# Moving copies, loads and late projections between queues and slots in a four-layer sandwich kernel

## The reference, cut to what matters

```
x = x + layernorm(layer(layernorm(x)))
```

```
gate = silu(lin(x, w1q, a1, b1)); up = lin(x, w3q, a3, b3); y = lin(gate * up, w2q, a2, b2)
lin(x, wq, A, B) = x @ tile(wq, (1, 4)).T + 0.5 * x @ A.T @ B.T
```

```
q = x @ Wq; k, v = x @ Wkv; w = softmax(causal(q k^T) / sqrt(32)); y = (w v) @ Wo + bo
```

## Time and profile before

| | |
|---|---|
| Median of three runs (lowest, highest) | 2157.19 us (2152.95, 2161.05) |
| The profiled execution | 2154.8 us, span 2153.0 us |
| TensorE busy, granted clock | 2002.1 us (93%), 0.973 of full |
| VectorE, GpSimd, ScalarE busy | 1423.2 (66%), 1064.7 (49%), 933.4 us (43%) |
| DMA | 292 MB, mean 136 GB/s |

### The profile page before, as it was taken

The page is one execution under the profiler, slowest core; times in us unless marked ns, Lnnn a source line. Parts: engine busy times, 40 slices in busy tenths (PEclk is TensorE's granted clock), DMA queues, the critical chain, the costliest instruction groups (busy, mean ns, idle before and its releaser), DMA issues. The chain is left out here.

```text
span 2153.0 us, 30681 instructions
## 1 busy us (share of the span) xinstructions
PE 2002.1 (93%) x10444; PEld 1451.0 (67%) x10444; DVE 1423.2 (66%) x3201; ACT 933.4 (43%) x1938; POOL 1064.7 (49%) x914
## 2 busy tenths in 40 slices
PE   5889886999999999989999899999998999999998
PEld 4644545778788878855666466665654687888887
DVE  7877667777777763177776477677776677654433
ACT  5645685333333323115554455555555433323211
POOL 1444586666666530008886488688884343220000
PEclk9999988999999999989999999999998999999999
DMA  6400376244444338532334643433253385543432
GB/s 188 173 9 1 121 232 230 94 151 167 162 167 167 123 129 305 156 95 57 79 81 111 188 117 80 113 98 97 64 165 117 95 271 183 180 168 132 142 123 97
DMA packets 153435, 292.12 MB, mean 136 GB/s; under 512 B 28750, under 2 KB 69582, under 8 KB 153152
## 3 DMA queue, kind: packets, MB, share of 16 engines
q1 hardware_dynamic: 124224, 241.93, 35.4%
q10 hardware_dynamic: 29056, 48.24, 6.8%
HBM read 163.48 MB, written 94.90 MB: 120 GB/s over the span
## 5 line engine op out<-in xcount | busy, mean ns | idle before, releaser
L2253 ACT ACTIVATE c_P<-PS 128x512 f32<-128x512 f32 (+3 forms) x768 | 349.1, 496 | 342.0 <-PE PS L2086 193.2
L2068 PE MATMUL PS<-c_K,c_Q 96*128 96x512 f32 (+3 forms) x768 | 276.8, 371 | 20.2 <-DVE cst L2385 8.8
L2086 PE MATMUL PS<-c_Q,c_K 97*128 97x512 f32 (+3 forms) x768 | 275.7, 373 | 17.1 <-ACT c_P L2253 9.8
L2498 POOL TENSOR_TENSOR c_S<-c_S,c_P 128x1024 f32<-128x1024 f32 (+3 forms) x94 | 242.0, 2575 | 20.3 <-DVE c_S L2334 12.9
L2086 PEld LDWEIGHTS PS<-c_Q,c_K 97*128 97x128 f32 x768 | 147.4, 193 | 140.0 <-ACT c_P L2253 96.3
L2381 DVE TENSOR_REDUCE cst<-PS 128x1 f32<-128x512 f32 x256 | 175.8, 687 | 77.0 <-PE PS L2068 76.7
L2068 PEld LDWEIGHTS PS<-c_K,c_Q 96*128 96x128 f32 x768 | 149.9, 195 | 77.0 <-DVE cst L2385 28.8
L214 POOL TENSOR_TENSOR maskw<-maskw,mhalf 128x1 f32<-128x1 f32 x64 | 37.7, 590 | 329.9 <-DVE maskw L172 317.6
L1432 DVE SCALAR_TENSOR_TENSOR b_pr<-b_g,b_a 128x460 f32<-128x460 f32 x192 | 180.8, 977 | 1.7
L2385 DVE CUSTOM_DVE_ANT_0 PS<-PS,maskw,cst 128x128 f32<-128x128 f32 (+3 forms) x256 | 142.8, 558 | 53.2 <-PE PS L2068 34.0
L2475 POOL TENSOR_SCALAR_AFFINE_SELECT c_P<-c_P 128x512 f32<-128x512 f32 x128 | 87.4, 683 | 159.8 <-ACT c_P L2253 159.8
(11 more groups left out here) (305 smaller groups left out, 4845.5 us busy)
## 6 DMA issues: line engine op xcount, KB each, us to landing
pre_d<-b_pre ACTq DMA_DIRECT2D x36, 512.0 KB, 2.8
c_w<-pre_d SPq DMA_DIRECT2D x34, 512.0 KB, 4.0
a_xin<-in_x SPq DMA_DIRECT2D x32, 512.0 KB, 4.3
d_x<-scr SPq DMA_DIRECT2D x32, 512.0 KB, 4.8
c_Q<-c_qh SPq DMA_DIRECT2D x240, 64.0 KB, 2.0
scr<-a_xin SPq DMA_DIRECT2D x16, 512.0 KB, 5.7
b_xn<-scr SPq DMA_DIRECT2D x16, 512.0 KB, 6.7
b_x<-scr SPq DMA_DIRECT2D x16, 512.0 KB, 5.8
```

Source lines behind the costliest of these rows:

```text
L2068: e.matmul(bank[:, 0:hi - lo], self.Q4[0:96, 4 * (o % 3) + g, 128 * t:128 * t + 128], self.K4[0:96, HEADS[o % 8], lo:hi], start=True, stop ...
L2086: e.matmul(self.k.bank(i % 3)[:, 0:hi - lo], self.K4[0:97, HEADS[o % 8], 128 * kt:128 * kt + 128], self.Q4[0:97, 4 * (o % 3) + g, lo:hi], ...
L2253: e.activation(self.P[:, R % 3, g, 0:hi - lo], self.k.bank(i % 3)[:, 0:hi - lo], ACT.Exp, scale=SCALE).then_inc(self.exp_s.s, 1)
L2498: e.tensor_tensor(S[:, gs, 512 - n:512], S[:, gs, 512 - n:512], P[:, gs, 0:n], ADD).then_inc(self.psum_s.s, 1)
```

## The change

Stage B: ScalarE's high copy of a weight part moves behind the other work of its chunk, and GpSimd's subtraction behind its two adds. Stage C: the weight loads inside the rounds and the output weights' loads go from SP's queue to ScalarE's, at the same slots, behind the exponential and the job's copy; those of the output product come every 8 slots instead of 6. K2's second half, job 7, K3 and job 11 get later slots and places, the reloads others; the finish steps of the odd half before slots 240 to 287 come 5 later, and the product of that half in round 5 at r = 7 instead of r = 4. Stage D's early tiles start 3 and 2 slots later, and its copies and subtractions move by 1 to 3 slots. The functions `sp_w` and `sp_wo` are renamed `load_w` and `load_wo`; their calls before the rounds stay on SP (left out below).

```diff
--- before.py
+++ after.py
@@ -1342,8 +1342,6 @@
                 if last is not None:
                     self.act_pre_store(e, last)
                 self.act_silu(e, t, c)
-                if p is not None:
-                    self.act_pre_hi(e, p)
                 if c in (0, 2):
                     self.act_ghi(e, t - 1, c // 2)
                 if t == 1 and c < 3:
@@ -1359,6 +1357,8 @@
                         self.act_low(e, t + 1)
                 if t > 1 and c == 4:
                     T.act_x(e, t - 2)
+                if p is not None:
+                    self.act_pre_hi(e, p)
                 if now is not None:
                     self.act_pre_load(e, now)
                 if t == 1 and c == 5:
@@ -1549,12 +1549,12 @@
                     T.pool_y(e, t - 1)
                 if t + 1 < NT and c == 3:
                     self.pool_xsum(e, t + 1)
+                self.pool_gf(e, t, c)
                 p = self.pre_at(t, c, 1)
+                if t > 1 and c == 3:
+                    T.pool_x(e, t - 2)
                 if p is not None:
                     self.pool_pre_lo(e, p)
-                self.pool_gf(e, t, c)
-                if t > 1 and c == 3:
-                    T.pool_x(e, t - 2)
                 if t == 1 and c < 3:
                     self.w2lo(e, 2 * c)
         T.pool_x(e, 14)
@@ -1593,19 +1593,19 @@
 
 JOBS = [("K0", None, None), ("K1", None, None), (0, None, None), (1, None, None), (2, None, None)]
 JOBS += [q_job(3), q_job(4), q_job(5), (6, q_slots(172, 2, 190, 2), (194, 206)),
-         ("K2", q_slots(208, 1, 219, 1), (217, 228)), (7, q_slots(231, 1, 243, 1), (242, 260)), q_job(8), q_job(9), q_job(10),
-         ("K3", q_slots(405, 1, 416, 1), (414, 425)), (11, q_slots(428, 1, 438, 2), (437, 454)), q_job(12), q_job(13),
+         ("K2", q_slots(208, 1, 220, 1), (218, 233)), (7, q_slots(235, 1, 247, 1), (245, 262)), q_job(8), q_job(9), q_job(10),
+         ("K3", q_slots(407, 1, 418, 1), (416, 427)), (11, q_slots(430, 1, 441, 2), (439, 457)), q_job(12), q_job(13),
          q_job(14), q_job(15)]
 JOB = {job[0]: n for n, job in enumerate(JOBS)}
 
-RELOAD = [239 + 2 * n for n in range(4)] + [255 + 2 * n for n in range(4)] + [263 + 3 * n for n in range(8)]
-WO_IN = {644 + 6 * c: c for c in range(8)}
-TILES = {711 + 4 * n: (0, n) for n in range(8)} | {745 + 4 * n: (1, n) for n in range(5)}
+RELOAD = [244 + 2 * n for n in range(4)] + [256 + 2 * n for n in range(4)] + [264 + 2 * n for n in range(8)]
+WO_IN = {644 + 8 * c: c for c in range(8)}
+TILES = {714 + 4 * n: (0, n) for n in range(8)} | {747 + 4 * n: (1, n) for n in range(5)}
 
 LAST = [(14, r) for r in range(7, 12)] + [(15, r) for r in range(6, 12)]
 
@@ -1800,7 +1800,7 @@
         e.dma_start(self.raws[n], self.k.io["wv"][:, 128 * n:128 * n + 128].rearrange("(c p) n -> p c n", p=128)
                     ).then_inc(self.wld[n].s, 16)
 
-    def sp_w(self, e, m, half):
+    def load_w(self, e, m, half):
 
         if m >= len(JOBS) - 1:
             return
@@ -1819,7 +1819,7 @@
             e.wait_ge(*self.half_s(self.last_of(2 if m == 4 else m - 1) + 1))
         e.dma_start(self.piece(m, half)[:, :, :].bitcast(F32), self.k.pre_d[self.stored(m, half)]).then_inc(self.wld[half].s, 16)
 
-    def sp_wo(self, e, c):
+    def load_wo(self, e, c):
 
         done, p = self.wld[c % 2], PRE.index(("wo", c, 0))
         e.wait_ge(*self.qmm_s(2 * len(JOBS)))
@@ -1912,7 +1912,7 @@
 
     def finish_at(self, S, step):
 
-        late = 5 if S >= 720 or 432 <= S < 480 else 0
+        late = 5 if S >= 720 or 240 <= S < 288 or 432 <= S < 480 else 0
         first, second = ((S - f[step] - d) // 48 if (S - f[step] - d) % 48 == at else -1
                          for f, at, d in zip(self.FINISH, (16, 0), (0, late)))
         return 2 * first if first >= 0 else 2 * second - 1 if second > 0 else None
...
@@ -1973,10 +1973,6 @@
                     self.sp_mrow(e, o + 1)
                 if S in self.place_at:
                     self.sp_place(e, *self.place_at[S])
-                if S in self.next_at:
-                    self.sp_w(e, *self.next_at[S])
-                if S in WO_IN:
-                    self.sp_wo(e, WO_IN[S])
                 if S in (692, 724, 746):
                     self.then.sp_first(e, S)
         self.sp_finish(e, 30, 4)
@@ -2298,17 +2294,21 @@
                     self.act_evac(e, 2 * o, 0)
                 if S in self.evac_at:
                     self.act_job(e, *self.evac_at[S])
+                if S in self.next_at:
+                    self.load_w(e, *self.next_at[S])
+                if S in WO_IN:
+                    self.load_wo(e, WO_IN[S])
                 if S in RELOAD:
                     self.act_reload(e, RELOAD.index(S))
                 if s == 39 and o < 15:
                     self.act_mrow(e, o + 1)
                 if S in (699, 701):
                     self.then.act_hi(e, 0, (S - 699) // 2)
-                if S in (727, 743):
-                    self.then.act_hi(e, 1, int(S > 727))
+                if S in (728, 744):
+                    self.then.act_hi(e, 1, int(S > 728))
                 if S == 758:
                     self.then.act_y(e, 0)
-                if S == 760:
+                if S == 762:
                     self.then.act_hi(e, 2, 0)
         self.act_evac(e, 31, 0)
 
@@ -2426,16 +2426,16 @@
                 for n in {708: [0], 712: [1], 716: [2], 720: [3], 724: [4], 747: [5], 751: [6], 757: [7], 761: [8]}.get(S, ()):
                     for g in range(4):
                         self.dve_last(e, n, g)
-                if S == 704:
+                if S == 707:
                     for half in range(2):
                         self.then.dve_lo(e, 0, half)
-                if S in (729, 744):
-                    self.then.dve_lo(e, 1, int(S > 729))
-                if S == 746:
+                if S in (730, 745):
+                    self.then.dve_lo(e, 1, int(S > 730))
+                if S == 748:
                     self.then.dve_y(e, 0)
                 if S == 755:
                     self.then.T[0].dve_y_nm(e, 0)
-                if S == 762:
+                if S == 764:
                     self.then.dve_lo(e, 2, 0)
         for n in (9, 10):
             for g in range(4):
@@ -2474,7 +2474,7 @@
                 if lo == 128 * kt:
                     e.affine_select(out=P[:, :, 0:128], in_=P[:, :, 0:128], compare_op=ALU.is_ge, fill=0.0, base=0,
                                     pattern=[[0, 4], [1, 128]], channel_multiplier=-1).then_inc(self.diag_s.s, 1)
-                if o > 0 and r in ((0, 7) if o in (9, 15) else (0, 4)):
+                if o > 0 and r in ((0, 7) if o in (5, 9, 15) else (0, 4)):
                     self.pool_mul(e, 2 * o - (2 if r == 0 else 1))
                 if (o, r) == (15, 7):
                     self.then.T[0].pool_y(e, 0)
```

More of the change, by code:

```diff
@@ L1934, in sp_first @@
         elif i == 2:
-            self.sp_w(e, 0, 0)
-            self.sp_w(e, 0, 1)
+            self.load_w(e, 0, 0)
+            self.load_w(e, 0, 1)
             self.sp_x(e, 4)
@@ L1945, in sp @@
             if u == 11:
-                self.sp_w(e, 1, 0)
-                self.sp_w(e, 1, 1)
-        self.sp_w(e, 2, 0)
+                self.load_w(e, 1, 0)
+                self.load_w(e, 1, 1)
+        self.load_w(e, 2, 0)
         for n in (0, 1):
@@ L1951, in sp @@
                 self.sp_place(e, n, part)
-        self.sp_w(e, 2, 1)
+        self.load_w(e, 2, 1)
         self.sp_place(e, 2, 0)
-        self.sp_w(e, 3, 0)
-        self.sp_w(e, 3, 1)
+        self.load_w(e, 3, 0)
+        self.load_w(e, 3, 1)
         self.sp_place(e, 2, 1)
-        self.sp_w(e, 4, 0)
+        self.load_w(e, 4, 0)
         self.sp_place(e, 3, 0)
-        self.sp_w(e, 4, 1)
-        self.sp_w(e, 5, 0)
+        self.load_w(e, 4, 1)
+        self.load_w(e, 5, 0)
         self.sp_place(e, 3, 1)
```

## The result

The changed kernel takes 2185.61 us (median of 4, 2183.48 to 2189.11) against 2155.70 for the kernel before on the same chip: ratio 1.0137 (1.0112 to 1.0162), some 30 us slower where 17.6 faster was forecast.

What follows compares the result with a forecast made beforehand. TensorE bounds the kernel, so only its waits and half clock can be won: -2.4 - 9.8 + 0.9 + 1.5 - 3.3 - 4.5 = -17.6 us, from 2154.8 profiled to 2137.2, about 2139.5 as median; range 2130 to 2150.

Steps and rivals of the forecast that it cites:

- gated layer: The copy out of xT's way gains 4 us, a new silu wait costs 1.6: net -2.4 us (-4 to 0).
- Rounds 4 and 5: Attention stage: waits and half clock worth 14.0 go, new waits of 1.2 and 3.0 come: -9.8 us (-15 to -4).
- Slot 240's wait of 5.12: Round 4: the row of maxima is issued some 7.5 us earlier, so this wait and 3.3 of half clock go.
- The new wait at slot 276: Round 5: job 7's second place lands late, so TensorE waits 3.0 us (0 to 6).
- rival (a): Waits are replaced: slot 276 waits 6 us with the clock falling, also at 672 and 711; 2149.5 us, chance 0.13.
- Rounds 8 and 9: K3 and job 11 later: job 11's second place comes some 0.8 later, +0.9 us (0 to 2.5).
- Loads on ScalarE's queue: 43 load issues may each delay the next exponential by about 0.45 us; low end taken, +1.5 us of 0 to 19.
- Slot 672: Start of round 14: row issued about 0.7 earlier, wait of 1.37 shrinks, two thirds of half clock go: -3.3 us.
- Slots 704 to 711: Round 14's end: the last maxima go first, 3.24 of wait and 1.3 of half clock go: -4.5 us (-1.5 to -6.5).
- the slower side: The whole kernel measures slower than before by over 0.5%: chance 0.05.
- the 43 issues: Rival: every load issue on ScalarE's queue delays TensorE; 2157 us at 0.45 each, 2168 from 0.7 each; chance 0.08.
- The 32 us: All the change can reach: TensorE's waits and half clock, 14.0 + 4.7 + 6.3 + 3.5, and small waits with them.

Runs made afterwards that it cites:

- e1: The kernel before with only the gated layer's two moves (ScalarE's copy, GpSimd's subtraction): 2191.32 us, ratio 1.0157.
- e5: e1 with the weight load's wait for its store's landing moved to the next copy, timed once: 2155.76 us.
- e7: e1 with the store behind the silu and the load's wait for the store's landing moved to the next copy: 2156.73 us, ratio 0.9995.
- e2: The changed kernel with the gated layer's two orders put back: 2150.37 us, ratio 0.9968.
- e8: The kernel before with 27 weight loads and 16 output weight loads issued on ScalarE's queue, at the same slots: 2153.88 us, ratio 0.9985.
- e9: The changed kernel with both edits of e7, K3 and job 11 at the slots of before, reloads and output weight loads at other slots: 2144.10 us, ratio 0.9942.
- e10: The kernel before with only the change's slots from 704 on: 2148.99 us, ratio 0.9962.
- e6: e1 with the weight part's store issued behind the silu of its step: 2166.75 us.

## Why the prediction was wrong

**The step that failed** is the last sentence but one on the gated layer: "The load behind it, which waits for the store's landing, comes 1.7 later too, but its silu and xT still end about 0.8 ahead of the fold." It holds for the load that is followed by xT. In the last of a step's six chunks L234 and the next tile's first silu stand behind the load instead, with 0.8 us of room. There, in the step shown, the store goes 2.5 later and lands 1.6 later still, with SP's two loads now ahead of it, and L234 waits 4.32 for it. And a late first silu makes the next copy, subtraction and store late, which the forecast of one step by itself couldn't show. Term: -2.4 forecast, +33 measured (e1). Its other sums were near: what the silu pays for standing behind the subtraction was forecast at 1.6 us (0 to 3.6) for twelve steps, and e5 less e7 is 2.5 in eleven; and the 4 us for the copy out of xT's way are 2.9 to 4.4 by e7's 303.1, against 305.9 to 307.4 in the four traces with before's gated layer.

**Rounds 4 and 5**: -9.8 forecast, -5.5 measured (116.5 to 111.0; 114.4 in e2, so the size is unsure). Slot 240's wait of 5.12 went, as told. The new wait at slot 276 was 2.80, forecast 3.0, but the clock did not fall behind it, where rival (a) had it fall: it fell for 6.8 us behind a wait that the forecast didn't have, at slot 261, and for 3.4 behind one at slot 231. Of TensorE's three waits of over 1 us there,

```profile
1210.41 0.50 PE L2064 MATMUL PS<-c_K,c_Q 96*128 96x512 f32 x1 [1.31 <-DVE cst L2385]
1246.14 0.69 PE L2064 MATMUL PS<-c_K,c_Q 96*128 96x384 f32 x1 [2.72 <-DVE cst L2385]
1263.94 0.30 PE L2064 MATMUL PS<-c_K,c_Q 96*128 96x128 f32 x1 [2.80 <-issue]
```

the second is that at slot 261, where the reciprocal stands in VectorE's queue for the sums' read, and the maxima behind it. The window behind it, and the rest of round 5:

```profile
1245.50:1252.30 6.80, 6.16 (x33) 3.41 (x33) 4.06 (x13) 3.05 (x6) 2.59 (x2) 0.50 0.53 160
1252.30:1276.20 23.90, 20.61 (x113) 12.53 (x110) 13.95 (x37) 9.74 (x23) 20.41 (x11) 1.00 0.77 232
```

I had followed the chain's DMAs to the product, not what queues behind the reciprocal.

**Rounds 8 and 9**: +0.9 forecast, +7.3 measured, by the same omission. In round 9 of the changed kernel, VectorE, then SP:

```profile
1441.54 0.26 DVE L2390 RECIPROCAL cst<-cst 128x16 f32<-128x16 f32 x1 [3.88 <-DMA cst<-sum_d]
```

```profile
1435.74 0.58 SPq L1907 DMA_DIRECT2D ctxT<-c_cH  x1
1436.36 0.53 SPq L1891 DMA_DIRECT2D sum_d<-c_cS  x1
1439.95 0.35 SPq L1896 DMA_DIRECT2D cst<-sum_d  x1
```

The later place puts the sums' write at slot 450 instead of 448; ScalarE's queue has issued a weight load 1.1 us ahead of it (1435.29), where on SP it had stood 0.6 behind. The write takes 3.6 us until its read can go, 1.8 before. TensorE waits 2.01 at slot 453 and the clock falls behind it. e8 and e9, with the queue but before's slots, keep 45.8, so the queue alone doesn't do it; the slots alone were not tried.

**Loads on ScalarE's queue**: +1.5 forecast, -3.4 measured by the medians (e8). The issues did cost something, most of it in round 13 (4.2 us in slots 640 to 655 of e8, 1.9 in the changed kernel, with the half clock behind them), and SP's relief is worth more than I let it have (5.2 in round 5). **Slot 672**: -3.3 forecast; the wait grew from 1.37 to 5.20 and round 13 from 43.7 to 48.5. Of the 3.8 more, 1.7 are the row's landing (6.0 instead of 4.3) and 2.1 its issue, 5.4 us behind the start of slot 664 instead of 3.3: the four reads ahead of it on SP's queue go only at 1642.98 for a write issued at 1638.62, behind two loads of ScalarE's (before at 1605.94, for 1603.86). The row lands late under the loads whichever queue has them (5.1 in e8), and ScalarE, not being held by SP's waits, issues two of them 1.1 and 0.7 us ahead of the row instead of 0.6 behind:

```profile
1643.67 0.39 ACTq L1828 DMA_DIRECT2D c_xth<-pre_d  x1
1644.09 0.49 ACTq L1828 DMA_DIRECT2D c_xtl<-pre_d  x1
```

The Trainium skill (DMA: Bandwidth & Descriptors, Issuing engines are not separate DMA queues) has it that the DMAs of all issuing engines run on the same 16 DMA engines and interleave there. The traces agree: the row lands in 6.0 us under another queue's loads, and in 2.1 with none (e9).

**Slots 704 to 711**: -4.5 forecast, -9.6 measured as rounds 14 and 15 (e10: 7.7 and 1.9), -8.3 by the times. The wait at slot 710 and the 6.8 us of half clock behind it went whole, where I had counted 1.3 of 3.1, and round 15 gained too. Not all of the 7.7 is this: the seven traces with before's slots there have round 14 at 44.7 to 48.2, and the kernel before had another 6.8 us of half clock behind slot 672. The subtractions take 1.80 together instead of 4.74, as forecast.

None of the rivals was this one: the slower side had 0.05, for the 43 issues, which cost a few microseconds in places and no more, and the gated layer's range ended at zero. The 32 us that the prediction called within reach add to 28.5 by its own four terms; the rest were small waits that it didn't list.

## What to carry to other kernels

- A wait on a DMA's landing inside an in-order queue is a wait for all that stands behind it, in every position of the loop. Before moving the work that feeds such a transfer, list for each position what stands behind the wait and how much room it has; and put the wait at the instruction that overwrites the data, not at the one that comes first.
- When a transfer moves by a microsecond, ask which large transfers it now stands behind. Here standing behind one or two loads went with a store's landing of 6.4 instead of 4.8 us, a row's of 6.0 instead of 4.3 (2.1 with none), and a write that could be read after 3.6 instead of 1.8. For the row and the write SP's own order had kept the next loads behind them, and a second queue doesn't keep that order; in round 9 it took the later slots as well.
- The instruction that shows TensorE's longest waits may be an echo. Breaking each link by itself told the cause (e5, e6); breaking only the one that looks costliest (e6) gave back 24.7 us and pointed at the wrong link.

## What was not expected of the hardware

- GpSimd's subtraction takes 1.30 us on the average ahead of its two adds and 1.55 behind them (27 and 28 of them from 480 to 940 us); the medians are 1.29 and 1.67.
- TensorE's clock halved in stretches with hardly a wait ahead of them (round 14 of e9: waits of at most 0.6 us, mean clock 0.85; the same round of e10 has 0.96), and stayed at full behind the wait of 2.80 us at slot 276 of the changed kernel.
- Issuing one DMA on ScalarE's queue took 1.53 us (e8, at 1589.49; the median of these eight is 0.53), at the same time as one of 1.58 on SP's.
